# TensorE takes two expert units at a time in a fused attention and mixture-of-experts kernel

## Chip, cores and metric

The kernel runs on one core of a Trainium2 chip. The time is the device time of that core in microseconds (us); lower is better.

## The reference

The input is 128 sequences of 32 tokens with 128 features. Cut to what matters:

```
# cond:  pooled = softmax(masked scores) @ hidden, per sequence, divided by a count
# attn:  16 heads of 8, plus a rotary part shared by the heads, causal, then W_o
x = x + attn(cond(x))
# cond2: one of 64 matrices per sequence
c2 = x @ W[cat] + b[cat]
# gate:  sigmoid scores of 64 experts, best 4 of 8 groups, best 8 experts, weights cw
for e in range(64):
    hmid = silu(c2 @ We_gate[e]) * (c2 @ We_up[e])
    y += cw[:, e] * (hmid @ We_down[e])
y += silu(c2 @ Ws_gate) * (c2 @ Ws_up) @ Ws_down      # shared expert
x = x + y
```

The kernel computes all 64 experts for all tokens; the routing weight of an expert that was not chosen is zero.

## The kernel before

The 4096 tokens are cut into `NBLK` = 8 blocks of `TOK` = 512. Each block goes through `UNITS` = 33 units: unit p below 32 is a pair of experts (64 hidden features each, 128 partitions), unit 32 is the shared expert. Every engine has its own hand-written instruction list; `pipeline(unit)` calls the engine's `unit` for each block b and unit p, and the engines meet only through semaphores. While the units of block b run, the attention, the gating and the routing of block b + 1 (`following`) are worked off in 33 steps: in unit p every engine does step p + 5 (`AHEAD`) of the following block, and from unit 28 on steps 0 to 4 of the block after it.

Weights and activations are split into a high and a low part, so a product is three matmuls of 128 x 512 (`three`, all recorded at L1049). A unit on TensorE is three such triples and then its step:

- `gate(b, p)`: c x wg into the bank `G[p % 2]`. It waits for the semaphore `weighted`, up to unit p - 2.
- `down(b, p - 4)`: hid_hi, hid_lo x wd, added into bank Y, four units behind. It waits for `lo_ready`.
- `up(b, p)`: c x wu into the bank `U[p % 2]`. It waits for `hid_ready`, up to unit p - 2.
- `attention_step(p + 5)`.

The other engines answer in a fixed order:

- ScalarE: silu of the gate bank (L544), then the rounding of unit p - 1 to `hid_hi` (L556), then its step. In unit 5 the step is the exponentials of the attention (L426), with a load of its function table before and after; in steps 12 to 15 it copies the transposed probabilities to `pt_sb` (L374), in step 17 the transposed attention output (L434), in step 19 the tokens (L437), in step 21 two activations on the gate scores (L440, L444).
- VectorE: gate bank x combine weights `cwb` (L990, counts `weighted`), then times the up bank (L1008, counts `hid_ready`), then its step. Some routing rows stand between the two (`attention_half_step`).
- GpSimd: the rest `hid_lo` (L664, counts `lo_ready`), then its step.
- SyncE: loads of `cwb` for each unit, four buffers.

In unit 6 (`LENT`) the gate and the up use the banks A0 and A2 of the attention. What VectorE does per unit is written in this order:

```
nc.vector.tensor_mul(hid[:, slot(b, p), :], gate_bank(p)[:, :], cwb[:, p % NCW, :])   # L990
for step, blk in now:
    attention_half_step(step, blk)
dve.wait_ge(S["up_done"], b * NPAIR + p + 1)
...
nc.vector.tensor_mul(hid[0:n, slot(b, p), :], hid[0:n, slot(b, p), :], up)             # L1008
...
    attention_step(step, blk)
```

Of the kernel before, what the change touches and what calls it, by code (L numbers as in the profile page):

```python
# [27 lines left out]
NPAIR = E // 2  # L28
UNITS = NPAIR + 1
# [50 lines left out]
def adaln_attention_moe(nc, x_tok, x_feat, prompt, cats, cond_w, cond_b, weights, consts, gate_bias,  # L80
                        we_gate, we_up, we_down, ws_gu, ws_down, out):
    ctx = ExitStack()
    with ctx:
# [23 lines left out]
        NH = 4  # L107
# [71 lines left out]
        S = {}  # L179
# [22 lines left out]
        def steps_in(p, b, last=False):  # L202

            if last or b is None:
                return [(p + AHEAD, b)] if b is not None and p + AHEAD < STEPS else []
            return [(p + AHEAD, b)] if p + AHEAD < STEPS else [(p + AHEAD - STEPS, b + 1)]
# [10 lines left out]
        def pipeline(unit):  # L217

            for b in range(NBLK):
                following = b + 1 if b + 1 < NBLK else None  # L220
                for p in range(UNITS):
                    unit(b, p, b % 2, following, b == NBLK - 2, b > 0)

        def slot(b, p):

            return (b * UNITS + p) % NH
# [4 lines left out]
        def gate_bank(p):  # L231
            return A0 if p == LENT else U[0] if p == NPAIR else G[p % 2]

        def up_bank(p):
            return A2 if p == LENT else U[p % 2]
# [809 lines left out]
        def _(pe):  # L1045
            def mm(dst, lhsT, rhs, **k):
                k.setdefault("start", True)
                k.setdefault("stop", True)
                return nc.tensor.matmul(dst, lhsT, rhs, **k)  # L1049
# [239 lines left out]
            def three(dst, w_hi, w_lo, m_hi, m_lo, first, final):  # L1289

                mm(dst, w_hi, m_hi, start=first, stop=False)
                mm(dst, w_lo, m_hi, start=False, stop=False)
                return mm(dst, w_hi, m_lo, start=False, stop=final)

            def down(b, p):
                pe.wait_ge(S["lo_ready"], b * UNITS + p + 1)
                if b == 0 and p % 4 == 0:
                    pe.wait_ge(S["split_lo"], 3 * (p // 4) + 3 if p < NPAIR else NSPLIT + 1)
                if p == 0:
                    if b == 0:  # L1300
                        pe.wait_ge(S["weighted"], NPAIR + 1)
                    pe.wait_ge(S["y_ready"], b + 1)
                if p == NPAIR:
                    mm(Y[:, :], wd_hi[:, p, :], hid_hi[:, slot(b, p), :], start=False, stop=False)
                    last = mm(Y[:, :], wd_lo[0:F, p, :], hid_hi[0:F, slot(b, p), :], start=False, stop=True)
                else:
                    last = three(Y[:, :], wd_hi[:, p, :], wd_lo[:, p, :], hid_hi[:, slot(b, p), :], hid_lo[:, slot(b, p), :],
                                 p == 0, False)
                last.then_inc(S["down_done"], 1)

            def gate(b, p, par, following):
                if b == 0 and p % 4 == 0:
                    pe.wait_ge(S["split_lo"], 3 * (p // 4) + 2 if p < NPAIR else NSPLIT + 1)
                if p == LENT:
                    if following is not None:
                        pe.wait_ge(S["v_ready"], following * TILES + TILES)
                elif p == NPAIR:
                    pe.wait_ge(S["hid_ready"], b * UNITS + (p - 1))
                elif b == 0 and p in (2, 3, 4):
                    pe.wait_ge(S["silu_done"], p - 1)  # L1320
                elif b == 0 and p == 5:
                    pe.wait_ge(S["hid_ready"], 2)
                else:

                    pe.wait_ge(S["weighted"], (b + 1) * NPAIR + (p - 3 if p == LENT + 2 else p - 1))
                three(gate_bank(p)[:, :], wg_hi[:, p, :], wg_lo[:, p, :], c_hi[par][:, :], c_lo[par][:, :], True, True)\
                    .then_inc(S["gate_done"], 1)

            def up(b, p, par, following, prev):
                if p == LENT:  # L1330
                    if following is not None:
                        pe.wait_ge(S["score_read"], following * TILES + TILES - 1)
                elif b == 0 and p in (2, 3, 4, 5):
                    pe.wait_ge(S["weighted"], NPAIR + p - 1)
                elif p >= 2:

                    pe.wait_ge(S["hid_ready"], b * UNITS + (p - 3 if p == LENT + 2 else p - 1))
                elif p == 0 and prev:
                    pe.wait_ge(S["hid_ready"], b * UNITS)
                three(up_bank(p)[:, :], wu_hi[:, p, :], wu_lo[:, p, :], c_hi[par][:, :], c_lo[par][:, :], True, True)\  # L1340
                    .then_inc(S["up_done"], 1)

            def unit(b, p, par, following, last, prev):
# [27 lines left out]
                for step, blk in steps:  # L1371
                    attention_step(step, blk)

            pe.sem_inc(S["y_ready"], 1)
            pipeline(unit)
            for p in range(UNITS - NH, UNITS):
                down(NBLK - 1, p)

# [53 lines left out]
```

## Time and profile before

| | before |
|---|---|
| median of 2 runs | 719.25 us (718.66 to 719.85) |
| the profiled execution | 719.35 us |
| its span, first to last instruction | 717.5 us |
| TensorE busy | 695.1 us, 97% |
| VectorE busy | 549.4 us, 77% |
| ScalarE busy | 443.7 us, 62% |
| GpSimd busy | 423.1 us, 59% |

The busy time of TensorE rests on modelled ends of matmuls that overlap, so the distance between starts tells its pace better than the durations. The span leaves out 1.85 us around the first and the last instruction.

### The profile page before, as it was taken

To read this page: it belongs to the slowest core of one execution; us is meant where nothing else is said; L and a number is where in the kernel's file an instruction comes from. 1 tells how busy PE (TensorE), PEld (TensorE's weight loads), DVE (VectorE), ACT (ScalarE), POOL (GpSimd) and SP (SyncE) were. 2 spreads that over 40 slices of the span, in tenths; PEclk is the share of its full clock that TensorE was granted. 3 is DMA by queue.
4 is the path that set the end of the run, shared out by engine and by line. 5 is a ranking of instruction groups with operands and counts; after the bars stand their busy time and mean duration, and the time that the engine had idled before them with its cause. 6 is when DMAs were issued, how large, how long until landed. Compare 5 with 4: busy or idle time off the path is not lost.

```text
span 717.5 us, 15764 instructions
## 1 busy us (share of the span) xinstructions
PE 695.1 (97%) x5612; PEld 542.1 (76%) x5612; DVE 549.4 (77%) x1149; ACT 443.7 (62%) x857; POOL 423.1 (59%) x349
## 2 busy tenths in 40 slices
PE   8897998999999999999999999999999999999998
PEld 6665685677877778777787778877787777888886
DVE  5797769877697777887688866977878876887665
ACT  3866765577555855568455775558654685555554
POOL 3446778765466655566456655566555664566664
PEclk9999999999999999999999999999999999999999
DMA  8553644454543444435434474434464354346441
GB/s 282 167 190 104 169 104 112 97 143 132 113 128 108 137 125 122 126 108 161 120 103 126 124 152 108 130 108 147 105 131 141 93 152 116 108 116 164 128 132 49
DMA packets 65342, 92.96 MB, mean 130 GB/s; under 512 B 7729, under 2 KB 26929, under 8 KB 65265
## 3 DMA queue, kind: packets, MB, share of 16 engines
q1 hardware_dynamic: 61088, 86.96, 44.4%
q10 hardware_dynamic: 4176, 5.01, 2.0%
q8 instruction: 44, 0.72, 0.4%
q14 instruction: 34, 0.27, 0.1%
HBM read 88.40 MB, written 3.15 MB: 128 GB/s over the span
## 4 chain that ended last, share of the span: by engine, by line
PE 70%; DVE 12%; ACT 8%; issue 4%; SPq 3%; DMA 2%; DVEq 0%; POOL 0%; ACTq 0%
PE banks L1049 67%; DVE hid L990 3%; ACT banks L544 2%; DVE hid L1008 2%; ACT s_t L426 2%; PE banks L1129 1%; DVE k_blk L717 1%; DVE pt_sb L692 1%; ACT L544 1%; ACT L426 1%; SPq L316 1%; SPq L310 1%; ACT hid_hi L556 1%; DMA x_early<-in_x_feat 1%; SPq L359 1%
## 5 line engine op out<-in xcount | busy, mean ns | idle before, releaser
L664 POOL TENSOR_TENSOR hid_lo<-hid,hid_hi 128x512 fp32r<-128x512 f32 x255 | 331.4, 1300 | 249.9 <-ACT hid_hi L556 248.4
L990 DVE TENSOR_TENSOR hid<-banks,cwb 128x512 f32<-128x512 f32 x252 | 173.1, 687 | 114.1 <-ACT banks L544 111.1
L544 ACT ACTIVATE banks<-banks 128x512 f32<-128x512 f32 x252 | 146.2, 582 | 124.1 <-PE banks L1049 122.5
L556 ACT CAST hid_hi<-hid 128x512 fp32r<-128x512 f32 (+1 forms) x264 | 162.7, 616 | 82.7 <-DVE hid L1008 81.8
L1008 DVE TENSOR_TENSOR hid<-hid,banks 128x512 f32<-128x512 f32 (+1 forms) x262 | 179.8, 687 | 23.6 <-PE banks L1049 1.9
L1049 PE MATMUL banks<-c_hi,wg_hi 128*128 128x512 f32 x264 | 119.2, 452 | 4.0 <-DVE hid L990 3.8
L1049 PE MATMUL banks<-hid_hi,wd_hi 128*128 128x512 f32 x264 | 104.0, 394 | 1.0 <-POOL hid_lo L664 0.8
L1049 PE MATMUL banks<-hid_hi,wd_lo 128*128 128x512 f32 (+1 forms) x264 | 103.9, 394 | 0.0
L1049 PE MATMUL banks<-c_hi,wu_hi 128*128 128x512 f32 x256 | 102.0, 399 | 1.6 <-DVE hid L1008 1.6
L1049 PE MATMUL banks<-c_hi,wg_lo 128*128 128x512 f32 x264 | 103.4, 392 | 0.0
L1049 PE MATMUL banks<-c_lo,wg_hi 128*128 128x512 f32 x264 | 103.2, 391 | 0.0
L1049 PE MATMUL banks<-c_lo,wu_hi 128*128 128x512 f32 x256 | 100.1, 391 | 0.0
L1049 PE MATMUL banks<-hid_lo,wd_hi 128*128 128x512 f32 x256 | 100.1, 391 | 0.0
L1049 PE MATMUL banks<-c_hi,wu_lo 128*128 128x512 f32 x256 | 99.7, 390 | 0.0
L1049 PEld LDWEIGHTS banks<-c_hi,wg_hi 128*128 128x128 f32 x264 | 49.6, 188 | 24.7 <-DVE hid L990 7.9
L1049 PEld LDWEIGHTS banks<-c_hi,wu_hi 128*128 128x128 f32 x256 | 48.1, 188 | 16.8 <-DVE hid L1008 5.2
L1049 PEld LDWEIGHTS banks<-hid_hi,wd_hi 128*128 128x128 f32 x264 | 49.6, 188 | 13.2 <-POOL hid_lo L664 1.6
L1049 PEld LDWEIGHTS banks<-hid_hi,wd_lo 128*128 128x128 f32 (+1 forms) x264 | 49.6, 188 | 13.0 <-issue 2.7
L1049 PEld LDWEIGHTS banks<-c_lo,wg_hi 128*128 128x128 f32 x264 | 49.6, 188 | 10.7
L1049 PEld LDWEIGHTS banks<-c_hi,wg_lo 128*128 128x128 f32 x264 | 49.9, 189 | 8.8 <-issue 3.3
L1049 PEld LDWEIGHTS banks<-hid_lo,wd_hi 128*128 128x128 f32 x256 | 48.1, 188 | 10.7
L1049 PEld LDWEIGHTS banks<-c_lo,wu_hi 128*128 128x128 f32 x256 | 48.1, 188 | 10.4
(164 smaller groups left out, 812.6 us busy)
## 6 DMA issues: line engine op xcount, KB each, us to landing
cwb<-cw_scratch SPq DMA_DIRECT2D x254, 256.0 KB, 3.7
k_blk<-in_cond_w SPq DMA_DIRECT2D x112, 64.0 KB
xf<-in_x_feat SPq DMA_DIRECT2D x7, 256.0 KB, 3.9
out_feat<-y ACTq DMA_DIRECT2D x7, 256.0 KB, 3.9
wg_raw<-in_we_gate SPq DMA_DIRECT2D x3, 512.0 KB, 7.5
wu_raw<-in_we_up SPq DMA_DIRECT2D x3, 512.0 KB, 8.3
wd_raw<-in_we_down SPq DMA_DIRECT2D x3, 512.0 KB, 7.5
xf<-in_x_tok SPq DMA_DIRECT2D x6, 256.0 KB, 2.8
```

Source lines behind the costliest of these rows:

```text
L310: kinds.append(sp.value_load(cat_row[0:1, bass.ds(blk * SPB + s, 1)], min_val=0, max_val=CATS - 1))
L316: sp.dma_start((wcat_first if opening(blk) else wcat)[:, s, :], cond_w[bass.ds(kinds[s] * D, D), :]).then_inc(S["wcat_in"], 16)
L359: sp.dma_start(cwb[:, p % NCW, :], src).then_inc(cwb_in[p % NCW], 16)
L426: nc.scalar.activation(s_t[:, t, :], s_t[:, t, :], ACT.Exp, scale=ATT_SCALE)\
L544: nc.scalar.activation(dst, gate_bank(p)[:, :], ACT.Silu).then_inc(S["silu_done"], 1)
L556: nc.scalar.copy(hid_hi[0:n, slot(b, p), :], hid[0:n, slot(b, p), :]).then_inc(S["hi_ready"], 1)
L664: nc.gpsimd.tensor_sub(rest, hid[0:n, slot(b, p), :], hid_hi[0:n, slot(b, p), :].bitcast(F32)).then_inc(S["lo_ready"], 1)
L692: last = nc.vector.tensor_mul(rot[:, i, :].rearrange("p (s t) -> p s t", t=SEQ), ps[rows, :].rearrange("p (s t) -> p s t", t=SEQ), C["rota ...
L717: nc.vector.tensor_scalar(k_blk[:, h, :], A1[:, :], C["head_of_group"][:, h:h + 1], None, ALU.mult)\
L990: nc.vector.tensor_mul(hid[:, slot(b, p), :], gate_bank(p)[:, :], cwb[:, p % NCW, :])\
L1008: nc.vector.tensor_mul(hid[0:n, slot(b, p), :], hid[0:n, slot(b, p), :], up).then_inc(S["hid_ready"], 1)
L1049: return nc.tensor.matmul(dst, lhsT, rhs, **k)
```

## The change

In blocks 1 to 7 TensorE takes two units at a time: both gates, both downs of four units back, both ups, then the attention steps of both units one after the other. Unit 32 stays alone, block 0 as it was. Each call keeps the waits that it had. The lists of VectorE, ScalarE and SyncE are unchanged, and so is the number of matmuls.

```diff
+            def down_behind(b, p, prev):
+                if p >= NH:
+                    down(b, p - NH)
+                elif prev:
+                    down(b - 1, UNITS + p - NH)
+
+            def two_units(b, p, par, following, last, prev):
+                if p % 2 and p < NPAIR:
+                    return
+                both = [q for q in (p, p + 1) if q < UNITS and (p < NPAIR or q == p)]
+                if p == 0:
+                    pe.wait_ge(S["c_lo_ready"], b + 1)
+                for q in both:
+                    gate(b, q, par, following)
+                for q in both:
+                    down_behind(b, q, prev)
+                for q in both:
+                    if q < NPAIR:
+                        up(b, q, par, following, prev)
+                for q in both:
+                    for step, blk in steps_in(q, following, last):
+                        attention_step(step, blk)
+
+            def either(b, p, par, following, last, prev):
+                (two_units if prev else unit)(b, p, par, following, last, prev)
+
             pe.sem_inc(S["y_ready"], 1)
-            pipeline(unit)
+            pipeline(either)
```

**First place**, TensorE in block 1, units 22 to 25, which have no attention step on TensorE; wg, wu and wd are the gate, up and down weights. Before, from the up of unit 22: up 22, gate 23, down 19, up 23.

```order
635 L1049 MATMUL banks<-c_hi,wu_hi 128x512 [waits hid_ready]
636 L1049 MATMUL banks<-c_hi,wu_lo 128x512
637 L1049 MATMUL banks<-c_lo,wu_hi 128x512
638 L1049 MATMUL banks<-c_hi,wg_hi 128x512 [waits weighted]
639 L1049 MATMUL banks<-c_hi,wg_lo 128x512
640 L1049 MATMUL banks<-c_lo,wg_hi 128x512
641 L1049 MATMUL banks<-hid_hi,wd_hi 128x512 [waits lo_ready]
642 L1049 MATMUL banks<-hid_hi,wd_lo 128x512
643 L1049 MATMUL banks<-hid_lo,wd_hi 128x512
644 L1049 MATMUL banks<-c_hi,wu_hi 128x512 [waits hid_ready]
645 L1049 MATMUL banks<-c_hi,wu_lo 128x512
646 L1049 MATMUL banks<-c_lo,wu_hi 128x512
```

The same engine now, from the up of unit 22: up 22, up 23, gate 24, gate 25. In front of these rows stand the gates of units 22 and 23 and the downs of units 18 and 19.

```order
641 L1049 MATMUL banks<-c_hi,wu_hi 128x512 [waits hid_ready]
642 L1049 MATMUL banks<-c_hi,wu_lo 128x512
643 L1049 MATMUL banks<-c_lo,wu_hi 128x512
644 L1049 MATMUL banks<-c_hi,wu_hi 128x512 [waits hid_ready]
645 L1049 MATMUL banks<-c_hi,wu_lo 128x512
646 L1049 MATMUL banks<-c_lo,wu_hi 128x512
647 L1049 MATMUL banks<-c_hi,wg_hi 128x512 [waits weighted]
648 L1049 MATMUL banks<-c_hi,wg_lo 128x512
649 L1049 MATMUL banks<-c_lo,wg_hi 128x512
650 L1049 MATMUL banks<-c_hi,wg_hi 128x512 [waits weighted]
651 L1049 MATMUL banks<-c_hi,wg_lo 128x512
652 L1049 MATMUL banks<-c_lo,wg_hi 128x512
```

Between the up of an even unit and the gate three units on there were six triples; now there are two. Between a gate and the gate two units on, which uses the same bank, there are still five.

**Second place**, TensorE in block 1 around step 17 (transposes of the attention output, L1154) and step 18 (the product with W_o, `h_feat,w`). Before, from the transposes: a whole unit stands between the two steps.

```order
537 L1154 MATMUL banks<-c,att 128x128 [waits att_ready]
538 L1154 MATMUL banks<-c,att 128x128 x3
539 L1049 MATMUL banks<-c_hi,wg_hi 128x512 [waits weighted]
540 L1049 MATMUL banks<-c_hi,wg_lo 128x512
541 L1049 MATMUL banks<-c_lo,wg_hi 128x512
542 L1049 MATMUL banks<-hid_hi,wd_hi 128x512 [waits lo_ready]
543 L1049 MATMUL banks<-hid_hi,wd_lo 128x512
544 L1049 MATMUL banks<-hid_lo,wd_hi 128x512
545 L1049 MATMUL banks<-c_hi,wu_hi 128x512 [waits hid_ready]
546 L1049 MATMUL banks<-c_hi,wu_lo 128x512
547 L1049 MATMUL banks<-c_lo,wu_hi 128x512
548 L1049 MATMUL banks<-h_feat,w 128x512 [waits attT_ready]
```

Now step 18 stands right behind step 17, and its wait for the ScalarE copy (`attT_ready`) with it:

```order
546 L1154 MATMUL banks<-c,att 128x128 [waits att_ready]
547 L1154 MATMUL banks<-c,att 128x128 x3
548 L1049 MATMUL banks<-h_feat,w 128x512 [waits attT_ready]
549 L1049 MATMUL banks<-c_hi,wg_hi 128x512 [waits weighted]
550 L1049 MATMUL banks<-c_hi,wg_lo 128x512
551 L1049 MATMUL banks<-c_lo,wg_hi 128x512
552 L1049 MATMUL banks<-c_hi,wg_hi 128x512 [waits weighted]
553 L1049 MATMUL banks<-c_hi,wg_lo 128x512
554 L1049 MATMUL banks<-c_lo,wg_hi 128x512
```

Steps 5 and 6, 13 and 14, 15 and 16, 19 and 20, 31 and 32 have moved together in the same way. In the other pairs at most one of the two steps has work on TensorE.

## Rows read from the trace of the kernel before

**Rows 1.** The page: busy time and share, and TensorE's clock in 40 slices.
```profile
PE 695.1 (97%) x5612; PEld 542.1 (76%) x5612; DVE 549.4 (77%) x1149; ACT 443.7 (62%) x857; POOL 423.1 (59%) x349
PEclk9999999999999999999999999999999999999999
```

**Rows 2.** Waits of TensorE: total us, times, longest.
```profile
PE banks L1049 <- DVE hid L990: 3.8, 7, 1.8
PE banks L1049 <- DVE hid L1008: 1.6, 6, 0.3
```

**Rows 3.** Timeline of TensorE, rope product of two blocks: start, duration, instruction.
```profile
398.00 0.45 PE L1049 MATMUL banks<-k_rope,rope_sum 32*32 32x32 f32 x32
...
482.43 0.45 PE L1049 MATMUL banks<-k_rope,rope_sum 32*32 32x32 f32 x32
```

**Rows 4.** Timeline of all engines, units 29 to 32 of a block.
```profile
389.98 0.69 DVE L1008 TENSOR_TENSOR hid<-hid,banks 128x512 f32<-128x512 f32 x1
...
390.70 0.62 ACT L556 CAST hid_hi<-hid 128x512 fp32r<-128x512 f32 x1 [0.26 <-DVE hid L1008]
...
391.02 0.39 PE L1049 MATMUL banks<-c_hi,wg_hi 128*128 128x512 f32 x1
...
391.40 1.30 POOL L664 TENSOR_TENSOR hid_lo<-hid,hid_hi 128x512 fp32r<-128x512 f32 x1 [1.10 <-ACT hid_hi L556]
...
393.06 0.39 PE L1049 MATMUL banks<-c_hi,wg_hi 128*128 128x512 f32 x1
```

**Rows 5.** Timeline of VectorE and TensorE around the gate of unit 9.
```profile
418.25 0.69 DVE L1008 TENSOR_TENSOR hid<-hid,banks 128x512 f32<-128x512 f32 x1
418.85 0.69 DVE L990 TENSOR_TENSOR hid<-banks,cwb 128x512 f32<-128x512 f32 x1
...
419.59 0.50 PE L1049 MATMUL banks<-c_hi,wg_hi 128*128 128x512 f32 x1
```

**Rows 6.** Timeline at the end of block 7: VectorE waits for TensorE.
```profile
710.81 0.39 PE L1049 MATMUL banks<-hid_lo,wd_hi 128*128 128x512 f32 x1
...
711.31 0.69 DVE L1008 TENSOR_TENSOR hid<-hid,banks 64x512 f32<-64x512 f32 x1 [0.69 <-PE banks L1049]
```

**Rows 7.** Timeline of TensorE at the first up of a block.
```profile
396.21 0.50 PE L1049 MATMUL banks<-c_hi,wu_hi 128*128 128x512 f32 x1 [0.27 <-DVE hid L1008]
396.55 0.39 PE L1049 MATMUL banks<-c_hi,wu_lo 128*128 128x512 f32 x1
```

**Rows 8.** Timeline of VectorE: rope mask, one score tile, then the total.
```profile
398.53 0.29 DVE L721 TENSOR_TENSOR rope_mask<-banks,c 128x128 f32<-128x128 f32 x1 [0.20 <-PE banks L1049]
...
404.74 0.68 DVE L738 TENSOR_TENSOR s_t<-banks,rope_mask 128x512 f32<-128x512 f32 x1
...
406.06 0.68 DVE L971 TENSOR_TENSOR y<-banks,y 128x512 f32<-128x512 f32 x1
```

**Rows 9.** Timeline of ScalarE: the rounding of unit 4.
```profile
410.88 0.62 ACT L556 CAST hid_hi<-hid 128x512 fp32r<-128x512 f32 x1
```

**Rows 10.** Timeline of TensorE and ScalarE, steps 13 and 17.
```profile
418.56 0.63 PE L1129 MATMUL banks<-c,s_t 128*128 128x128 f32 x4 [0.27 <-ACT pt_sb L374]
...
430.64 0.60 PE L1154 MATMUL banks<-c,att 128*128 128x128 f32 x4
...
431.00 0.48 PE L1049 MATMUL banks<-c_hi,wg_hi 128*128 128x512 f32 x1
...
431.28 0.59 ACT L434 COPY h_feat<-banks 128x512 f32<-128x512 f32 x1 [0.70 <-PE banks L1154]
```

**Rows 11.** Timeline of TensorE and ScalarE, step 21.
```profile
441.89 1.00 PE L1049 MATMUL banks<-w,c 128*128 128x64 f32 x8
...
442.93 0.38 ACT L440 ACTIVATE score<-banks 128x256 f32<-128x256 f32 x1 [1.11 <-PE banks L1049]
```

**Rows 12.** Timeline of VectorE: four maxima of the routing, and the rotation.
```profile
458.48 0.60 DVE L833 MAX8 best<-biased 128x8 f32<-128x64 f32 x4
...
472.20 1.38 DVE L692 TENSOR_TENSOR pt_sb<-banks,c 64x512 f32<-64x512 f32 x2
```

## Prediction

> **What bounds the kernel now.** Start with the page: the busy shares and the granted clock [rows 1]. TensorE is busy 97% of the span at full clock, VectorE 77%, ScalarE 62%. Busy alone says little for a pipelined engine, so next the list of waits, cut to TensorE [rows 2]: waits for `weighted` (VectorE L990) come to 3.8 us and for `hid_ready` (VectorE L1008) to 1.6 us in the whole run. The matmul stream is the bound and its partners answer in time. The period of a block with attention steps is read between two rope products, 398.00 and 482.43: 84.43 us [rows 3]. Then the timeline of one unit without attention work [rows 4]: gate to gate is 2.04 us, so one triple of matmuls (gate, down or up) takes 0.68 us and one matmul 0.227 us. The question is therefore not how much work TensorE has, which the change leaves alone, but how long it gives the others to answer.
>
> **The slack of the answers.** Call g, d, u the three triples. A gate waits for the VectorE product of two units back, w (L990, `weighted`), and an up for the second one, h (L1008, `hid_ready`). VectorE takes its work in the order w(p), h(p), steps of p, w(p+1), h(p+1), and h(p) cannot start before u(p) ends. So w(p+1) sits in the queue behind u(p), though its own input is long there. Before, u(p) is followed by g, d, u(p+1), g, d, u before g(p+3) would come: seven triples after the start of u(p), 4.8 us. Now, for even p, u(p) is followed by u(p+1), g(p+2) and at once g(p+3), which needs w(p+1). From the start of u(p), TensorE gets there in three triples, 2.04 us, plus the attention steps between. The answer takes: third matmul of u(p) at 0.45; VectorE starts 0.50 after such a matmul, 710.81 to 711.31 [rows 6]; that is h(p) at 0.95; w(p+1) 0.60 later and the gate 0.74 after w, 419.59 [rows 5]: 2.29 us. **The bare wait is 0.25 us a pair.** A wait also costs a restart: the matmul after 396.21 comes 0.34 later in place of 0.227 [rows 7], 0.11 more. So 0.36 us a pair with nothing else in it, and whatever VectorE does between h(p) and w(p+1), the steps of the even unit, adds in full. That work is free now.
>
> **One block with attention, pair by pair** (p is the unit, the step is p + 5):
> - Pair 0, 1: steps 5 and 6 now adjoin. Step 6 needs the rope mask: rope start to VectorE 0.53, its add 0.29, 0.06 to TensorE: 0.88, against 0.45 of the product itself [rows 3, 8]. With the restart **0.5**.
> - Pair 2, 3: step 8 needs the second score tile read, step 7 of VectorE, which stands behind h(2). h(2) at 0.95 after u(2), the add 0.60 later, read after 0.68 and 0.06: 2.29; TensorE is there after 1.36. Wait **0.9**. The total (L971, 0.60) lies before w(3), but the matmuls of step 8 cover it.
> - Pair 4, 5: step 9 of VectorE is an add and a maximum, 404.74 to 406.06, 1.32 [rows 8]. No product of TensorE covers it: 0.25 + 1.32 + 0.11 = **1.7**.
> - Pair 6, 7: ScalarE is at the exponentials with two table loads. From its rounding of unit 4 (410.88) to w(7) are 7.97 us [rows 5, 9], to g(9) 8.71. The rounding starts 0.72 after h(4) [rows 4], so g(9) comes no earlier than 1.67 + 8.71 = 10.4 after u(4). TensorE has in that stretch nine triples, 6.1, the wait above, 1.7, and the first transposes with their switch, 0.5: 8.3. Wait and restart **2.2**. Before, three more triples and step 13 stood there.
> - Pairs 8, 9 and 10, 11: transposes, values, and then something that needs ScalarE's copy of those transposes. Transposes to copy 0.64, copy 0.59, 0.06: 1.29 [rows 10], against some 0.5 of transposes and 0.5 of value products: 0.3 each, **0.6**.
> - Pair 12, 13: step 18 waits for the copy of step 17: 1.29 less the 0.36 of the transposes themselves, 430.64 to 431.00 [rows 10] = **0.9**. Pair 14, 15: the same with step 20 behind 19, **1.0** with the silu of unit 15 that stands behind that copy.
> - Pair 16, 17: silu(17) queues behind the two gate activations of step 21. 1.04 to the first, 0.8 for both by the 0.38 of one [rows 11], 0.6 silu, 0.74 for w: 3.2 from the start of the step; TensorE gets to g(19) after the step with the pooling behind it, 1.7 (its next gate was at 443.59), and a gate of 0.79. With the restart **0.9**.
> - Pairs 18 to 25: four pairs with routing on VectorE and no TensorE step. The four maxima of unit 22 take 0.60 [rows 12]; the steps of units 18, 20 and 24 lie on both sides of that. 0.25 + 0.6 + 0.11 = 1.0 each, **4.0**.
> - Pair 26, 27: the first products of the next block wait for ScalarE's copy of the combine weights: **0.5**.
> - Pair 28, 29: rotation, 1.38 [rows 12], ahead of w(29): 0.25 + 1.38 + 0.11 = **1.7**.
> - Unit 32: its gate needs h(30): 0.95 + 0.74 = 1.69 against 1.36: **0.4** with the restart.
>
> Sum: 0.5 + 0.9 + 1.7 + 2.2 + 0.6 + 0.9 + 1.0 + 0.9 + 4.0 + 0.5 + 1.7 + 0.4 = 15.3 us.
>
> **What it removes.** u(0) now stands behind two gates and two downs and no longer waits for unit 32: the stop of about 0.4 ahead of 396.21 and its restart go, 0.5 [rows 7]. The wait of 0.27 before the transposes at 418.56 [rows 10] with its restart, 0.35, goes into the terms above. Six times two steps stand side by side, and one change of tile shape falls away; the only rows for it are the restarts, 0.11 once or twice: 0.15 each, 0.9, with 0.7 to 1.4 as bounds. Together 1.7. Downs lose two triples of slack at most: from the start of u(30) to d(30) there are seven triples, 4.8, and h, rounding and the GpSimd rest need 0.95 + 0.72 + 0.70 + 1.3, 3.7 [rows 4]. No cost, bounds 0 and 0.3 a block. The loads of SyncE keep their order and wait for w of four units back, two pairs, over 8 us: nothing.
>
> Net 15.3 - 1.7 = 13.6 us a block. Six blocks (1 to 6) have the attention steps of the next: 6 x 13.6 = 82. Block 6 lacks steps 32 to 4, so it loses the rotation term, but silu(27) then stands uncovered for about as much. Block 7 has no step: 15 x 0.36 + 0.4 - 0.5 = 5.3. Block 0 is unchanged. **Sum 87 us.** The profiled execution took 719.35 us, the median is 719.25: the same within 0.1. 719.3 + 87 = **806 us**.
>
> **Bounds.** If the base wait is 0.25 shorter, ten pairs a block and the fifteen of block 7 lose it (19 us), and if merging saves 1.4, 3 us more: 784. If the VectorE steps of odd units count too in the crowded stretches (a maximum, a row of routing, some 2 us a block) it is 12 more, and 0.3 for downs gives 2: 820. Errors of my walk through a block go on top of it.
>
> **Rivals.**
> - *Only the attention steps wait.* If w(p+1) comes within the 2.04 us, the terms of pairs whose VectorE work has no TensorE step vanish, and 0.5 + 0.9 + 0.6 + 0.9 + 0.9 + 0.5 = 4.3 less 1.7 stays: 6 x 2.6 = 16, **735 us**. For it: the base wait of 0.25 is a small difference of large terms. Against it: the 1.32 and 1.38 of VectorE cannot fit into it. 6%; something between this and the forecast, 6%.
> - *Not slower.* The longer run of independent triples removes the wait at u(0) and the shape changes and nothing comes in their place: 6 x 1.7 + 0.5 = 11 less, **708 us**. It decides at one point: VectorE would have to pass from h(p) to w(p+1), and w to the gate, in 1.09 us, where the rows give 0.60 + 0.74. 2%.
> - *The waits feed each other.* Where late rounding delays w of the next pair, the queue does not recover within a pair: about a third more of the 15.3, 30 us, **836 us**. For it: ScalarE and VectorE are in one order each, and units 2 to 7 are crowded on both. Against it: VectorE is busy 77%, and it has a pair of 4.4 us or more for 2.8 us of w and h. 8%.
> - *The clock.* The granted clock is full in all slices, and no stretch shows the other level [rows 1]; the new waits of 1.6 and 2.1 us stand a few us apart. If matmuls of two pairs a block ran at half speed, 24 triples would take 0.68 more each, less the waits of 4 that they would cover: 12 x 6 = 74 more, **880 us**. 3%. [...]
>
> **How the numbers follow.** The forecast holds with 75% (785 to 828). The range for 8 in 10 is 780 to 832: 12% lie below and about 8 above, some of each inside the edges. A measurement of this kernel can tell about 2% (14 us) from no change. Slower by over 2%: the forecast, the two larger rivals and most of the two smaller, 97%. Within 2%: 2%. Faster: 1%.
>
> **What will show it.** In the profile after, VectorE L990 should lead TensorE's list of waits with tens of us where it has 3.8; the block period should be 98 us; a bare pair in block 7 should take 4.4 us in place of 4.08, with the gap before its second gate, nowhere else; step 18 should start some 1.3 after the transposes of step 17; the wait at u(0) should be gone; block 7 should be 5 us longer; VectorE's busy time should be the same 549 us. The prediction is wrong if the gap before g(p+3) is absent in bare pairs, or if downs begin to wait for GpSimd.

## The result and the profile after

The changed kernel takes 812.43 us (median of 2 runs, 810.29 to 814.58) beside 719.25: 1.1295 times as long, 95% interval 1.1161 to 1.143. The forecast was 806 us. The profiled execution took 810.29 us, its span is 808.4.

The page of the changed kernel: busy time of each engine, then TensorE's granted clock in 40 slices.

```profile
PE 723.7 (90%) x5612; PEld 544.7 (67%) x5612; DVE 541.2 (67%) x1149; ACT 443.1 (55%) x857; POOL 422.5 (52%) x349
PEclk9998999999999999999999999999999999999999
```

Against [rows 1]: every engine does the same number of instructions, VectorE and ScalarE are busy for as long as before or a little less, and all shares have fallen. Time was added, not work. TensorE's 724 in place of 695 us is not more work either: block 1, at full clock throughout, has 86.2 us of busy time where a block before has 83.9, from modelled ends of matmuls in front of gaps (a matmul is listed with 0.39 us where starts are 0.227 apart), and the next block, with a mean granted clock of 0.98, has 87.9.

The list of waits of the changed kernel, cut to TensorE: total us, times, longest.

```profile
PE banks L1049 <- DVE hid L990: 50.0, 56, 1.9
PE banks L1172 <- ACT att L437: 4.2, 6, 0.7
PE banks L1049 <- DVE s_t L738: 4.2, 6, 0.7
PE banks L1049 <- ACT h_feat L434: 4.0, 6, 0.7
PE banks L1049 <- DVE rope_mask L721: 3.0, 7, 0.4
PE banks L1049 <- ACT cw_feat L452: 2.8, 5, 0.6
```

The first line is the gates' wait for `weighted`, 3.8 us in [rows 2], now 50. The other five are attention steps that stand right behind the step whose answer they need, once a block (one in the opening comes on top for L721). The wait for L1008, 1.6 us before, is gone from the list.

The rope products of four blocks of the changed kernel give the period of a block, as [rows 3] did.

```profile
146.00 0.45 PE L1049 MATMUL banks<-k_rope,rope_sum 32*32 32x32 f32 x32
243.57 0.45 PE L1049 MATMUL banks<-k_rope,rope_sum 32*32 32x32 f32 x32
342.77 0.45 PE L1049 MATMUL banks<-k_rope,rope_sum 32*32 32x32 f32 x32
442.00 0.45 PE L1049 MATMUL banks<-k_rope,rope_sum 32*32 32x32 f32 x32
```

Block 1 takes 97.57 us, the next two 99.20 and 99.23, where it was 84.43. The forecast was 98.0 for each. What sets block 1 apart is the clock, a mean of 1.00 against 0.98 in each of the next two; more on it further down.

A bare pair in block 7 of the changed kernel, timeline of all engines:

```profile
752.70 0.50 PE L1049 MATMUL banks<-c_hi,wg_hi 128*128 128x512 f32 x1
...
754.14 0.58 ACT L544 ACTIVATE banks<-banks 128x512 f32<-128x512 f32 x1
...
754.87 0.39 PE L1049 MATMUL banks<-c_hi,wu_hi 128*128 128x512 f32 x1
...
755.75 0.69 DVE L1008 TENSOR_TENSOR hid<-hid,banks 128x512 f32<-128x512 f32 x1 [1.33 <-PE banks L1049]
...
756.23 0.39 PE L1049 MATMUL banks<-c_hi,wg_hi 128*128 128x512 f32 x1
756.36 0.69 DVE L990 TENSOR_TENSOR hid<-banks,cwb 128x512 f32<-128x512 f32 x1
...
757.10 0.50 PE L1049 MATMUL banks<-c_hi,wg_hi 128*128 128x512 f32 x1
```

Read it from the first matmul of up(p) at 754.87. h(p) starts 0.88 later, at 755.75, and in front of it VectorE has stood idle for 1.33 us; w(p+1) comes 0.61 behind it, at 756.36, and the second gate, g(p+3), 0.74 behind w, at 757.10. The first gate, 756.23, waited for nothing. Gate to gate a pair takes 757.10 - 752.70 = 4.40 us, in place of 2 x 2.04 = 4.08 [rows 4]. The silu that w(p+1) needs ended at 754.72, about 1.0 us before h(p) began. So VectorE was idle with the input of w(p+1) ready: the order of its queue, not the amount of its work, makes the wait.

### The profile page after: what moved, and what is told of

Same layout as the page of the kernel before. It is cut to its first block, busy times and chain, and to the rows that moved or that the text cites. A ratio compares the mean times of both kernels' runs of the same rounds, so it can differ in the third digit from the quotient of the medians.

```text
span 808.4 us, 15764 instructions
## 1 busy us (share of the span) xinstructions
PE 723.7 (90%) x5612; PEld 544.7 (67%) x5612; DVE 541.2 (67%) x1149; ACT 443.1 (55%) x857; POOL 422.5 (52%) x349
## 4 chain that ended last, share of the span: by engine, by line
PE 65%; DVE 17%; ACT 8%; issue 5%; SPq 2%; DMA 1%; DVEq 0%; POOL 0%; ACTq 0%; POOLq 0%
PE banks L1049 63%; DVE hid L990 5%; DVE hid L1008 4%; ACT s_t L426 2%; PE banks L1129 1%; ACT banks L544 1%; ACT pt_sb L374 1%; ACT L544 1%; ACT L426 1%; DVE pt_sb L692 1%; SPq L316 1%; SPq L310 1%; ACT hid_hi L556 1%; DVE s_t L738 1%; DVE best L833 1%
## 5 line engine op out<-in xcount | busy, mean ns | idle before, releaser
L1008 DVE TENSOR_TENSOR hid<-hid,banks 128x512 f32<-128x512 f32 (+1 forms) x262 | 179.9, 687 | 128.7 <-PE banks L1049 115.4
L990 DVE TENSOR_TENSOR hid<-banks,cwb 128x512 f32<-128x512 f32 x252 | 172.8, 686 | 99.2 <-ACT banks L544 94.9
L1049 PE MATMUL banks<-c_hi,wg_hi 128*128 128x512 f32 x264 | 125.5, 475 | 51.2 <-DVE hid L990 50.0
L1049 PEld LDWEIGHTS banks<-c_hi,wg_hi 128*128 128x128 f32 x264 | 49.7, 188 | 100.6 <-DVE hid L990 85.0
L1049 PE MATMUL banks<-hid_hi,wd_hi 128*128 128x512 f32 x264 | 106.0, 401 | 0.9 <-POOL hid_lo L664 0.7
L1049 PE MATMUL banks<-hid_hi,wd_lo 128*128 128x512 f32 (+1 forms) x264 | 106.0, 402 | 0.0
L1049 PE MATMUL banks<-c_lo,wg_hi 128*128 128x512 f32 x264 | 104.7, 397 | 0.0
L1049 PE MATMUL banks<-c_hi,wg_lo 128*128 128x512 f32 x264 | 104.5, 396 | 0.0
L1049 PE MATMUL banks<-hid_lo,wd_hi 128*128 128x512 f32 x256 | 101.9, 398 | 0.0
L1049 PE MATMUL banks<-c_hi,wu_hi 128*128 128x512 f32 x256 | 101.9, 398 | 0.0
L1049 PE MATMUL banks<-c_lo,wu_hi 128*128 128x512 f32 x256 | 100.1, 391 | 0.0
L1049 PE MATMUL banks<-c_hi,wu_lo 128*128 128x512 f32 x256 | 100.1, 391 | 0.0
L1049 PEld LDWEIGHTS banks<-hid_hi,wd_lo 128*128 128x128 f32 (+1 forms) x264 | 50.8, 193 | 14.1 <-issue 2.7
L1049 PEld LDWEIGHTS banks<-hid_hi,wd_hi 128*128 128x128 f32 x264 | 50.8, 192 | 14.1 <-POOL hid_lo L664 1.6
L1049 PEld LDWEIGHTS banks<-c_lo,wg_hi 128*128 128x128 f32 x264 | 50.1, 190 | 11.4
L1049 PEld LDWEIGHTS banks<-c_hi,wu_hi 128*128 128x128 f32 x256 | 48.6, 190 | 12.9 <-issue 1.7
L1049 PEld LDWEIGHTS banks<-hid_lo,wd_hi 128*128 128x128 f32 x256 | 49.3, 193 | 11.3
L1049 PEld LDWEIGHTS banks<-c_lo,wu_hi 128*128 128x128 f32 x256 | 48.4, 189 | 10.4
L1049 PEld LDWEIGHTS banks<-c_hi,wu_lo 128*128 128x128 f32 x256 | 48.6, 190 | 10.0
```

## The experiments

Each ratio is against runs of the kernel before on the same chip: 717.26 us for the order of block 7 alone, the extra copies and the steps alone; 717.57 for both moves together, the second form of VectorE's pairs and the last experiment; 718.1 for the other four. The changed kernel itself was measured only beside the 719.25 above, so differences from its 812.43 are good to about 2 us. Where an edit adds lines, line numbers move: L1049 is L1051 or L1063 there, and in the kernels with VectorE in pairs L990 is L985 and L1008 is L1022.

**Block 7 alone.**

```diff
-                (two_units if prev else unit)(b, p, par, following, last, prev)
+                (two_units if b == NBLK - 1 else unit)(b, p, par, following, last, prev)
```

> The changed order of TensorE in block 7 alone, where no attention step is left; blocks 0 to 6 as before. V: a wait of 0.25 and a restart of 0.11 per pair, 15 x 0.36 + 0.4 - 0.5 = 5.3 us: 724.6 us. S: nothing or a small gain, 719 us.

Measured 724.23 us, ratio 1.0096 (1.0073 to 1.012). From the transposes of the last combine weights, the same place in both, to the end of the span it is 721.6 - 630.37 = 91.2 us against 717.5 - 632.33 = 85.2 before: 6.0 us in block 7. No attention step is left there, so pairing alone costs, and the size fits the 5.3 us expected.

**One more VectorE copy in every even unit of block 7**, with the pairs and without them.

```diff
                 nc.vector.tensor_mul(hid[0:n, slot(b, p), :], ...)      # h(p); other lines left out
+                if b == NBLK - 1 and p % 2 == 0 and 2 <= p < NPAIR:
+                    nc.vector.tensor_copy(s_t[:, 0, :], s_t[:, 1, :])
```

> As the order of block 7 alone, with one more VectorE copy of 128 x 512 (scratch data, 0.6 us) between h(p) and w(p+1) of each even unit from 2 to 30 in block 7; its result is used by nothing. V: each copy adds in full to the wait, 15 x 0.6 = 9 us on top of the block 7 kernel: 733.6 us. If the wait were for something else (ScalarE, the up banks), it adds nothing: 724.6 us.

> The kernel before with the same 15 extra VectorE copies in block 7. V: six triples of cover hide them, 719.3 us. If VectorE's work as such were the bound in a block of units, 728 us.

Measured 727.53 with the pairs (ratio 1.0137, 1.0118 to 1.0156), 3.3 us above the kernel of block 7 alone and not the 9 us expected, and 717.41 without them (1.0009, 0.9989 to 1.0029). The timeline of the kernel with pairs tells why:

```profile
684.27 0.69 DVE L1008 TENSOR_TENSOR hid<-hid,banks 128x512 f32<-128x512 f32 x1 [1.72 <-PE banks L1051]
...
684.87 0.42 DVE L1015 COPY s_t<-s_t 128x512 f32<-128x512 f32 x1
...
685.21 0.69 DVE L990 TENSOR_TENSOR hid<-banks,cwb 128x512 f32<-128x512 f32 x1
...
685.95 0.50 PE L1051 MATMUL banks<-c_hi,wg_hi 128*128 128x512 f32 x1 [0.36 <-DVE hid L990]
```

The copy holds VectorE for only 0.34 us (684.87 to 685.21), not 0.6, and the gate moves by nearly that: pairs of this kernel are 4.74 us long (681.21 to 685.95), those of the kernel of block 7 alone 4.42, 0.32 less. Work between h(p) and w(p+1) adds in full, and costs nothing where six triples cover it. My price of the copy was wrong, the mechanism was not. Fifteen copies make 15 x 0.32 = 4.8 us; from the same transposes to the end this run takes 726.1 - 630.42 = 95.7, 4.5 longer. The medians of whole times differ by less, 3.3 us.

**The steps alone.**

```diff
+                if prev and p < NPAIR:
+                    steps = steps_in(p - 1, following, last) + steps_in(p, following, last) if p % 2 else []
```

> The kernel before, with gate, down and up of single units as they were; in blocks 1 to 7 only the attention steps of two units are taken together, behind the odd unit. Theory V (the product w(p+1) of VectorE stands behind h(p), which needs the up of unit p, and the next gate but one needs w(p+1)): the gates keep their six triples of cover, so only the waits between adjoining steps are left, 0.5 + 0.9 + 0.6 + 0.9 + 0.9 + 0.5 = 4.3 less 1.7 saved, 6 x 2.6 = 16: 735 us. Rival S (the adjoining attention steps are what costs): about 800 us. Rival C (the clock alone): about 719 us.

Measured 752.26 us (1.0485, 1.0467 to 1.0503), 35 us in place of the 16 expected; the period of a block is 90.25, that is 5.8 longer in place of 2.6. Part of it is a slip of mine: the 1.7 us that I took off hold the wait of up(0), which this kernel keeps. The largest part of the rest, 1.56 us a block with the restart, stands in one place, here in its timeline of TensorE:

```profile
434.14 0.39 PE L1049 MATMUL banks<-c_lo,wu_hi 128*128 128x512 f32 x1
435.82 0.50 PE L1049 MATMUL banks<-c_hi,wg_hi 128*128 128x512 f32 x1 [1.28 <-DVE hid L990]
```

This is the gate of unit 9. ScalarE's exponentials and their two table loads (1.28 us each) take 5.3 us in both kernels (411.52 to 416.83 before, 427.74 to 433.05 here). Before, the matmuls of step 13 stood ahead of this gate. Moved behind it, they leave a gap: 1.68 between the two starts, 1.45 too much. I had priced this wait as one of the gates; a part of it belongs to the steps as well.

**The steps back in their units.**

```diff
                     if q < NPAIR:
                         up(b, q, par, following, prev)
-                for q in both:
                     for step, blk in steps_in(q, following, last):
```

> The changed kernel, but each attention step stands behind the up of its own unit (up p, step, up p+1, step). V: the waits between adjoining steps shrink by 3.0 us a block (an up of 0.68 stands between), the six saved switches of 0.15 are given back, 6 x 2.1 = 13 us less than the changed kernel: 799 us. S: nearly all of the loss goes, about 725 us.

Measured 789.58 us (1.0994, 1.0975 to 1.1012), 23 less than the changed kernel where 13 were expected, and still 71 above before. So adjoining steps are the smaller part of the loss, though a larger one than forecast: the period is 95.65, with a fall of the clock in each of the six blocks (0.66 of full speed from 165 to 170 us in the first of them); moving them back saves 3.6 us a block at full clock and not 2.1, because the waits between adjoining steps don't shrink but go altogether: those for L434, L437 and L452 are no longer in the list. The list of waits keeps 45.0 us for L990.

**Downs ahead of the gates.**

```diff
+                for q in both:
+                    down_behind(b, q, prev)
                 for q in both:
                     gate(b, q, par, following)
-                for q in both:
-                    down_behind(b, q, prev)
```

> The changed kernel with the two downs ahead of the two gates of a pair (down, down, gate, gate, up, up). V: two more triples, 1.36 us, lie between the up of unit p and the gate of unit p + 3, so the bare wait goes and VectorE steps up to 1.1 us are covered; left 0.5 + 0.9 + 0.3 + 2.1 + 0.6 + 0.9 + 1.0 + 0.5 + 0.3 = 7.1 less 1.7 a block, 6 x 5.4 = 32: 751 us, and block 7 costs nothing. S: the time stays at 812 us.

Measured 773.27 us (1.0773, 1.0755 to 1.0791): 39 us back by moving two triples, without an instruction more or less. The wait for L990 falls to 12.0 us, and the mean granted clock is 1.000 where it was 0.987; the falls of the clock were some 6.5 of the 39 us. It is 22 us more than expected; two of the reasons are in its timeline of TensorE and list of waits.

```profile
417.89 0.40 PE L1049 MATMUL banks<-hid_lo,wd_hi 128*128 128x512 f32 x1
419.08 0.50 PE L1049 MATMUL banks<-hid_hi,wd_hi 128*128 128x512 f32 x1 [0.79 <-POOL hid_lo L664]
```

```profile
PE banks L1049 <- DVE hid L990: 12.0, 15, 1.8
PE banks L1049 <- POOL hid_lo L664: 6.0, 12, 0.8
PE banks L1129 <- ACT s_t L426: 4.3, 7, 1.7
```

The second down of a block, of unit 30, now waits for GpSimd: the cover moved to the gates was taken from the downs. The same shows in block 7, which was expected to cost nothing: its pairs take 4.23 us, less than 4.40 but not 4.08, and from its first gate to the end it takes 770.7 - 694.99 = 75.7 us against 717.5 - 644.22 = 73.3 before. And TensorE arrives earlier at the exponentials, 4.3 us.

**Both.** Downs ahead, and steps in their units.

> Downs ahead of the gates, and each attention step behind the up of its own unit. The two losses are separate, so the savings add: the period of 93.4 of downs_first less the 3.6 that the steps in place saved on the changed kernel (97.6 to 94.0 without the falls of the clock), 89.8 against 84.4: 6 x 5.4 = 32 and 4 for block 7 and the opening: 754 us. If both remove the same wait: 773 us.

Measured 761.86 us (1.0615, 1.0576 to 1.0655). The first two periods are 90.65 and 90.67, 0.9 over the 89.8 expected; the next three are 92.13 to 92.17, and the time is 8 us over the forecast. The clock is not the reason, it is granted in full (1.00) in all five. The extra 1.5 us lie among the routing steps, where waits for L1008 (0.34) and one more for GpSimd (0.37) turn up and the one for L990 is 0.59 in place of 0.30. The savings add only partly.

**VectorE in pairs too.** w(p), w(p+1), then h(p), h(p+1), with TensorE as in the changed kernel.

```diff
+                if prev and p < NPAIR:
+                    if p % 2 == 0:
+                        weigh(b, p)          # w(p) with its waits; its lines are left out here
+                        weigh(b, p + 1)
```

> The changed kernel, and VectorE takes pairs too in blocks 1 to 7: w(p), w(p+1), then h(p) with its steps, h(p+1) with its steps. V: the terms in which the gate waits for w(p+1) behind h(p) go (1.7 + 4.0 + 1.7 a block and all of block 7), the wait behind ScalarE's exponentials grows from 2.2 to 3.0; left 8.7 - 1.7 = 7.0 a block, 6 x 7.0 = 42: 761 us. S: the time stays at 812 us.

Measured 810.0 us (1.1305, 1.1239 to 1.1371): no gain, where 51 us were expected. Taken alone, this would speak against the theory. But its list of waits has changed its head:

```profile
PE banks L1063 <- DVE rope_mask L721: 17.2, 7, 2.8
PE banks L1063 <- DVE hid L985: 15.8, 14, 1.9
```

and the timeline of a block's start shows the cause, VectorE first, then TensorE:

```profile
446.44 0.69 DVE L985 TENSOR_TENSOR hid<-banks,cwb 128x512 f32<-128x512 f32 x1 [4.30 <-ACT banks L544]
447.05 0.68 DVE L1022 TENSOR_TENSOR hid<-hid,banks 128x512 f32<-128x512 f32 x1
447.64 0.28 DVE L721 TENSOR_TENSOR rope_mask<-banks,c 128x128 f32<-128x128 f32 x1
...
447.98 1.15 PE L1063 MATMUL banks<-k_blk,q_sb 32*32 32x128 f32 x64 [2.80 <-DVE rope_mask L721]
```

The gates' wait for w (L985 there) went from 50.0 to 15.8 us, as the theory says. Block 7, where nothing else is in the way, shows it bare. These are the gates of one pair and of the next in the timeline of TensorE:

```profile
759.95 0.39 PE L1063 MATMUL banks<-c_hi,wg_hi 128*128 128x512 f32 x1
...
760.63 0.39 PE L1063 MATMUL banks<-c_hi,wg_hi 128*128 128x512 f32 x1
...
764.03 0.39 PE L1063 MATMUL banks<-c_hi,wg_hi 128*128 128x512 f32 x1
...
764.71 0.39 PE L1063 MATMUL banks<-c_hi,wg_hi 128*128 128x512 f32 x1
```

A pair takes 4.08 us again, as unpaired units do, and the second gate stands 0.68 behind the first: the gap is gone with TensorE's order unchanged. From its first gate to the end block 7 takes 809.0 - 735.28 = 73.7 us, against 79.0 in the changed kernel and 73.3 before. This is the most direct evidence that VectorE's queue order makes the bare wait.

In the blocks with attention steps another wait takes its place: w(1) waits for its silu, which stands behind ScalarE's copies of step 5, and holds up h(0) and the rope mask. Behind it the clock falls a second time in each block: in the block of these rows it is 0.72 from 450 to 455 us, and 0.67 again from 470 to 475. So I left units 0 and 1 in the old order:

> As vector_pairs, but units 0 and 1 of a block keep VectorE's old order w, h, w, h. In the trace of vector_pairs TensorE waited 2.80 us for the rope mask, because w(1) now stood ahead of it and waited for a silu behind ScalarE's copies of step 5, and the clock fell twice a block. If that one place hid the gain: the wait is 0.4 again, one fall of the clock (1.6 us) goes, the period of a block falls from 99.2 to about 95, 6 x 4 = 24 us less than vector_pairs: 786 us, 773 us if the clock does not fall at all. If the product order was not the cause of the gates' waits, it stays at 810 us.

Measured 790.28 us (1.1002, 1.0968 to 1.1036), 20 us less than vector_pairs, where 24 were expected. The periods of its last four blocks are 94.8 and 96.2 in turn, the longer ones with a fall of the clock (0.66 from 455 to 460 us in one of them, 1.00 throughout the shorter ones). The score tile of step 7 now waits behind w(3) (11.2 us in six waits, 4.2 in the changed kernel), so this order too gives part of its gain back in a new wait.

**Filling the two long waits.** Matmuls without use, so that TensorE is not idle there.

```diff
+                    if following is not None and q == LENT + 1:
+                        pe.wait_ge(S["score_read"], following * TILES + TILES - 1)
+                        filler(A2, 6, par)      # 6 matmuls of 128 x 512 into a free bank
+                    if following is not None and q == LENT + 3:
+                        pe.wait_ge(S["hid_ready"], b * UNITS + 5)
+                        filler(U[0], 8, par)    # 8 of them
                     gate(b, q, par, following)
```

> The changed kernel with matmuls that nobody uses in the two long waits: 6 of 128 x 512 (1.4 us) before the gate of unit 7, 8 (1.8 us) before that of unit 9, into banks that are free there, blocks 1 to 6. If the fall of the granted clock to half for 3.4 us in blocks 2 to 5 comes from these waits, it goes and with it 4 x 1.6 = 6.6 us: 805 us and a mean clock near 1.00. If the fall has another cause, the clock stays at 0.98 and the time at 812 us or a little more.

Measured 802.64 us (1.1183, 1.1164 to 1.1202): 84 matmuls more, 10 us less. All its block periods are 97.6 to 97.7. In the rows below, the number behind the busy times is the mean granted clock of the window, as a share of full speed. First two windows of the changed kernel, block 2: 0.68 in the 5 us behind the wait of unit 9, full behind them.

```profile
266.00:271.00 5.00, 5.00 (x33) 3.82 (x36) 1.42 (x3) 0.61 (x2) 1.83 (x2) 0.68 0.62 181
271.00:340.00 69.00, 62.07 (x417) 46.76 (x411) 46.92 (x110) 33.47 (x62) 32.84 (x26) 1.00 0.35 95
```

Then 100 us of the kernel with the filler, which hold the same place of a block, at full clock:

```profile
240.00:340.00 100.00, 91.51 (x729) 69.42 (x727) 66.27 (x141) 53.06 (x104) 49.23 (x40) 1.00 0.39 108
```

Not all of the 10 us is this fall. Of the two profiled executions the one with the filler is 7.8 us shorter (800.6 against 808.4); 5.9 of that lie in the five block periods (488.4 against 494.3), and 2.1 in the opening, which the filler doesn't touch.

**One move on the kernel before.** The wait of up(0) that pairing removes can be removed without pairing.

```diff
+                if p == 0 and prev:
+                    for step, blk in steps:
+                        attention_step(step, blk)
+                    steps = []
                 if p < NPAIR and not ahead:
                     up(b, p, par, following, prev)
```

> The kernel before with one thing moved: in unit 0 of blocks 1 to 7 step 5 (value and rope products) stands ahead of up(0), so that the wait of up(0) for unit 32 is covered. The wait of 0.43 and its restart of 0.11 go in six blocks, the switches stay the same: 3 us less than before, 715 us beside 718. If up(0) only waits elsewhere (its h product is 1.4 us later and the rope mask stands behind it), 718 us or up to 721.

Measured 714.39 us beside 717.57, ratio 0.9951 (0.9937 to 0.9964), half a per cent. It is the fastest kernel of the study. Its timeline of TensorE:

```profile
393.93 0.45 PE L1049 MATMUL banks<-k_rope,rope_sum 32*32 32x32 f32 x32
394.31 0.50 PE L1049 MATMUL banks<-c_hi,wu_hi 128*128 128x512 f32 x1
...
477.87 0.45 PE L1049 MATMUL banks<-k_rope,rope_sum 32*32 32x32 f32 x32
```

The up starts 0.38 behind the rope product and has no wait; the period is 83.94 in place of 84.43, 0.5 us a block as forecast.

## Why the prediction was right

**The base wait** was forecast at 0.25 + 0.11 us a pair; the bare pair shows 4.40 - 4.08 = 0.32. The one number a little off is VectorE's start after an up, 0.88 in place of 0.95 [rows 6]. Block 7 was forecast at 5.3 us longer; from its first gate to the end it is 808.4 - 729.37 = 79.0, 5.7 us longer than 73.3. With VectorE's order changed as well, the bare wait is gone (4.08).

**The block, term by term.** I read the waits off the starts of TensorE's timeline from 437 to 537 us, as the distance of two starts over the usual one, with the restart. The rows of the largest ones and of two steps, changed kernel:

```profile
449.21 1.06 PE L1049 MATMUL banks<-k_blk,q_sb 32*32 32x128 f32 x57 [0.70 <-DVE s_t L738]
...
455.13 0.39 PE L1049 MATMUL banks<-c_lo,wg_hi 128*128 128x512 f32 x1
456.85 0.50 PE L1049 MATMUL banks<-c_hi,wg_hi 128*128 128x512 f32 x1 [1.34 <-DVE hid L990]
...
461.29 0.40 PE L1049 MATMUL banks<-c_lo,wg_hi 128*128 128x512 f32 x1
463.63 0.67 PE L1049 MATMUL banks<-c_hi,wg_hi 128*128 128x512 f32 x1 [1.94 <-DVE hid L990]
464.10 0.63 PE L1049 MATMUL banks<-c_hi,wg_lo 128*128 128x512 f32 x1
464.52 0.63 PE L1049 MATMUL banks<-c_lo,wg_hi 128*128 128x512 f32 x1
...
481.32 0.60 PE L1154 MATMUL banks<-c,att 128*128 128x128 f32 x4
482.60 1.12 PE L1049 MATMUL banks<-h_feat,w 128*128 128x512 f32 x2 [0.68 <-ACT h_feat L434]
```

The gate of unit 7 comes 1.72 behind the matmul ahead of it in place of 0.227: 1.49, and 0.11 for the restart (the next starts 0.34 behind it, at 457.19). The gate of unit 9: 2.34, that is 2.11 over. Step 18 starts 1.28 after the transposes of step 17; 1.29 was forecast, against 0.36 [rows 10].

| units | forecast | measured |
|---|---|---|
| 0, 1: rope mask | 0.5 | 0.4 |
| 2, 3: score tile | 0.9 | 0.9 |
| 4, 5: maximum on VectorE | 1.7 | 1.6 |
| 6, 7: exponentials | 2.2 | 2.2 |
| 8 to 11: copies of transposes | 0.6 | 0.65 |
| 12, 13: step 18 | 0.9 | 0.9 |
| 14, 15: step 20 | 1.0 | 0.9 |
| 16, 17: gate activations | 0.9 | 0.8 |
| 18 to 25: routing | 4.0 | 3.4 |
| 26, 27: copy of the weights | 0.5 | 0.55 |
| 28, 29: rotation | 1.7 | 1.7 |
| 32 | 0.4 | 0.4 |
| sum | 15.3 | 14.4 |

The routing term was sized by one row for four pairs; the first of them has only 0.4. Less the savings, the block of full clock is 97.57 - 84.43 = 13.1 longer, 13.6 was forecast. The wait of up(0) is gone, as forecast.

**The clock** is what the forecast gave 3% and what came true in part. After 464.10 the next matmul starts 0.42 later, not 0.227: the granted clock from 464.10 to 467 us is 0.50 of full speed. The fall begins with the gate that waited 1.94 us, 6.8 us behind the gate that waited 1.34, or some matmuls behind it, once in each of blocks 2 to 5, and its price is the difference of two periods, 99.20 - 97.57 = 1.6 us. I had priced this rival at 12 us a block, with half speed through two pairs of every block. Both the half and the length were my assumptions: the trace of before has full clock throughout, and no run shows two pairs at half speed. The trace after shows the half, for eight or nine matmuls in each of four blocks. The filled waits show that these idle stretches take part in it: with them filled, the periods lose those 1.6 us. They are not enough by themselves. Block 1 has the same two waits, and keeps full clock (0.33 and 0.24 us from start to start behind the second wait):

```profile
160.85 0.50 PE L1049 MATMUL banks<-c_hi,wg_hi 128*128 128x512 f32 x1 [1.34 <-DVE hid L990]
...
167.62 0.50 PE L1049 MATMUL banks<-c_hi,wg_hi 128*128 128x512 f32 x1 [1.93 <-DVE hid L990]
167.95 0.39 PE L1049 MATMUL banks<-c_hi,wg_lo 128*128 128x512 f32 x1
168.19 0.40 PE L1049 MATMUL banks<-c_lo,wg_hi 128*128 128x512 f32 x1
```

Block 6 does the same (1.34 and 1.92; the clock is 1.00 from 660 to 670 us). What tells these two blocks from the four others stays open. The fall comes behind idle stretches (0.68 above) and goes when they are filled (1.00); that alone doesn't tell why blocks 1 and 6 were spared, and no run here shows the condition for a fall. In the opening, which no kernel here changes, the clock fell in the profiled runs of nine of the thirteen kernels (from 60 to 80 us it is 0.83 in the changed one) but not in that of the kernel before. The price of a lower mean clock in the kernel before is small: of 37 executions of the kernel before beside the experiments, the 14 with a mean clock of 0.999 or more take 717.2 us on average, the 10 with 0.996 or less 718.0.

**The sum.** Five periods are 72.1 us longer (494.3 between the first and the sixth rope product, 422.2 before), of which the clock has 6.5, some 1.6 in each of four blocks. From the sixth rope product to the end it is 17.5 longer, ahead of the first 1.3. Together 90.9, the difference of the spans. Without the clock 84.4 were left of the forecast 87. The forecast was right by its terms. That 806 came as near to the profiled 810.3 as it did is in part luck, since two errors of some 3 and 6 us had opposite signs; the median of 812.4 lies 2 us higher because the other of the two runs took 814.58.

**The rivals.** "Only the attention steps wait" is refuted as a whole, since the bare pairs wait too; but its part of the loss was priced too low: the steps alone cost 35 us, not 16, since the wait for the exponentials is partly theirs. "The waits feed each other" did not come true: the pairs measure what each was forecast alone. "Not slower" falls with the kernel of block 7 alone, 7.0 us slower. Downs waiting for GpSimd, named as a risk, happened only where the downs were moved ahead.

Left open: what brings the extra waits into the later blocks of the kernel with both moves, why the clock was spared in blocks 1 and 6, and how much of the 22 us that downs_first takes over its forecast belongs to the waits for GpSimd and how much to the exponentials.

## What to carry to other kernels

Before regrouping work on the bound engine, count for each wait the work that stands between the instruction that feeds the answering queue and the one that needs the answer, in both orders, and look for what stands in front of it in that queue: here six triples of cover became two, and VectorE's free time did not help because it was idle in front of the wrong instruction. Price each pair by what stands in the queue at that point, not by a mean. A change of order in one queue can be answered by the same change in the other, but look at what the answer moves: here it cured block 7 and brought new waits to the others. A single wait that a trace of the bound engine shows may be filled by moving one step; here that gave half a per cent without touching the rest.

## What was not expected of the hardware

- The granted clock fell to half (0.50 from 464.10 to 467 us) after two waits of TensorE of 1.3 and 1.9 us, 6.8 us apart, with matmuls between them, and stayed there for eight or nine matmuls of 128 x 512 (most of them 0.43 us apart, not 0.227). It did so in blocks 2 to 5 and not in blocks 1 and 6, with the same waits. In vector_pairs, with a wait of 2.8 us at the start of the block as well, it fell twice a block (0.72 from 450 to 455 us and 0.67 from 470 to 475).
- 14 matmuls a block that nobody uses took that fall away (1.00 from 240 to 340 us in clock_filler), 5.9 us over five block periods.
- A VectorE copy of 128 x 512, from one tile of `s_t` to another, took the engine 0.34 us in the kernel with extra copies (684.87 to 685.21), the product ahead of it, of the same size, 0.60 (684.27 to 684.87).
